# Cross attention whose shift rows carry the logarithm of the row sums, with the order of the work written out anew

## The chip, the core and the metric

The kernel runs on one core of a Trainium2 chip. The metric is the device time of one execution in microseconds (us), the median over runs. The core's engines work side by side, each through its own list of instructions, strictly in the order of that list: TensorE (PE in the rows; PEld is its loading of weights), VectorE (DVE), ScalarE (ACT), GpSimd (POOL) and SyncE (SP). They wait for one another through semaphores. A transfer is started ("issued") by an instruction in the list of SP or ACT and lands later.

## The reference

For 8 batches of 512 tokens with 512 features there are two blocks. The change is in the first, the cross attention over 77 context rows, with 16 heads of 32 features:

```python
q = (Q @ Wq).reshape(b, nq, H, dh).transpose(0, 2, 1, 3)      # Q = layernorm(x)
k = (K @ Wk)...; v = (V @ Wv)...                              # K = V = ctx_1024
S = einsum('bhqd,bhkd->bhqk', q, k) / sqrt(dh)
S = where(key_pos < valid_lens, S, -1e20)
A = softmax(S, axis=-1)
O = einsum('bhqk,bhkd->bhqd', A, v)
x = x + O.reshape(b, nq, d) @ Wo
```

The second block is a self attention over the 512 tokens, whose q, k, v and output weights get a low-rank part picked by a gate for each batch (two of eight experts); its result is added to x as well. Everything is float32.

## The kernel before

**The order.** Every piece of work is a step with a name and indices: `("csc", b, i, t)` is the cross scores of batch b, head group i, token tile t. A table, `CALENDAR` (L43 to L104), gives each kind of step a time for each of its indices; the step of batch b lies at `b * PERIOD + time`, with a period of 2034 units. A second table, `OWN` (L109 to L255), overrides single steps, mostly of the first and of the last batch. All steps are sorted by these times (`calendar`, L282), and each engine walks the sorted list and issues its part of each step (`Engine.walk`, L479). So the tables decide the order on each engine and nothing else; the units are not microseconds. Since three batches are under way at once, a step of batch b at time t lies among steps of batch b-1 at t + 2034 and of batch b-2 at t + 4068. The banks of PSUM and the slots of buffers are dealt out in the same order (`banks`, `ring`, L414 to L455).

**Cross attention of one batch** goes by four head groups i, of four heads each:

- `q1` (4 products) makes q; `q1_split` (ACT, DVE) splits it into a rounded part and a rest, so that the products that follow can run in the faster rounded format; `q1_rows` (ACT) and `q1_stack` (SP's transfers) put the parts under each other in a stack of rows (`cross_stack`, L584), one below the other: parts of q, a mask row, two shift rows.
- `csc` (L1255), four token tiles t: TensorE multiplies stack by keys, tokens on partitions, 4 heads x 78 columns; DVE takes the negated maximum of each row (L1040) into `negmax`.
- `cross_shift` (L1285): TensorE transposes `negmax`; DVE splits the 16 rows into a rounded part and a rest (L1051); `cross_shift_move` (L907): ACT issues two transfers that put them as shift rows under the stack.
- `csT` (L1292): TensorE multiplies again, now with keys on partitions, 99 rows deep, so that mask and maximum are already subtracted by the product itself; ACT takes the exponential into `probs1` (L914).
- `cpv` (L1305): probabilities by values, four products side by side on 32 columns each. `cden` (L1315): the same product with ones in place of the values, which gives the row sums on the partitions where the result stands.
- `cacc` (L928, ACT) copies the result out; `cinv` (L1078, DVE) takes the reciprocal of the row sums in four parts; `cdivide` (L757, POOL) multiplies the two, in one piece for i = 0 to 2 and in four for i = 3.
- `out1` (L1234): product with Wo, which waits for `cdivide`; `residual1` (L1084) adds it to x. Then come the second layer norm, the transposes `xpose`, the gate and the self attention: `weff`, `qk`, `v`, `sc`, `shift`, `shift_move`, `sT`, `pv`, `psum`, `den`, `inv`, `divide`, `out2`.

The self attention has shift rows of the same kind (`shift`, `shift_move`), and divides at the end (`den`, `inv`, `divide`). The two kinds of reciprocal share a ring of two buffers `inv_sum`. The score banks `sc` and `scT` have two buffers each, shared by cross and self attention, and the next score product in a bank waits until DVE or ACT has read the one before. `warm` steps multiply something that nobody reads, in the first batch alone.

Of the kernel before, what the change touches and what calls it, by code (L numbers as in the profile page):

```python
# [28 lines left out]
ROWS = SHIFT_ROW + 2  # L29
SIDE = 32  # L30
# [5 lines left out]
PJ_BANKS = 3  # L36
JUNK = 8
# [18 lines left out]
    "pick": (326,),
    "uv_load": (346, 397, 524, 2882),
    "csc": (-1491, -1471, -1462, -1458, -1042, -1041, -1018, -1014, -706, -696, -678, -673, -324, -308, -296, -277),
    "cross_shift": (-1369, -1007, -613, -257),
    "cross_shift_move": (-1320, -990, -595, -190),  # L60
    "csT": (-1253, -1237, -1208, -1190, -922, -921, -912, -880, -538, -500, -494, -473, -138, -137, -127, -84),
    "cpv": (-1128, -692, -415, -47),
    "cacc": (-1106, -626, -363, -44),
    "cden": (-963, -556, -444, -35),
# [1345 lines left out]
```

## Time and profile before

| | |
|---|---|
| median of 3 runs | 1420.75 us (1419.51 to 1426.21) |
| span of the profiled execution | 1426.7 us |
| TensorE busy | 1391.0 us, 97% |
| VectorE, ScalarE, GpSimd busy | 67%, 60%, 48% |
| mean granted TensorE clock | 0.98 of full |
| time from one batch to the next, batches 2 to 6 | 163.8 to 164.0 us |

The span of the profiled execution is 5.95 us longer than the median and 0.5 us longer than the longest of the three runs. How to read the rows further below: busy time is the time in which at least one instruction of a group runs, so the groups of TensorE, whose products overlap in the pipeline, sum to more than the engine's own busy time. A line of TensorE's products counts a float32 product as two records. The chain of waits goes back from the last instruction, at each step to what released it.

### The profile page before, as it was taken

The numbers are of one execution on the slowest core, as the hardware profiler recorded it, in microseconds if no ns is written. First come the engines' busy times: TensorE is split into PE (matmuls) and PEld (weight loads), VectorE is DVE, ScalarE is ACT, GpSimd is POOL, SyncE is SP. The second block draws the span as 40 slices with busy tenths as digits, with TensorE's granted clock in tenths as the row PEclk, the third lists the DMA queues.
The fourth block names the chain that finished last, engine by engine and source line by source line (L and its number), as shares of the span: only waits on it lengthen the run. The fifth ranks groups of instructions, "written<-read, shape, count | busy, mean of one in ns | idle before, by whom it ended". The sixth has DMA issues, their size and how long they took to land.

```text
span 1426.7 us, 17122 instructions
## 1 busy us (share of the span) xinstructions
PE 1391.0 (97%) x5704; PEld 702.4 (49%) x5704; DVE 951.9 (67%) x1687; ACT 861.3 (60%) x1499; POOL 679.8 (48%) x411
## 2 busy tenths in 40 slices
PE   8998999999999999999999999999999999999987
PEld 5545444545455444555555445455545454444432
DVE  4454577766767677767777677767777677666572
ACT  2425474866577663975658664876648665565652
POOL 2011143545555362556445463555625455465675
PEclk9889999999999999999999999999999999999999
DMA  7514233522434224522234224332235323233210
GB/s 252 143 53 133 46 68 96 153 76 46 98 110 108 75 54 125 137 61 76 68 111 123 75 59 135 110 85 67 58 104 152 76 46 97 64 101 79 81 39 30
DMA packets 78767, 130.81 MB, mean 92 GB/s; under 512 B 26374, under 2 KB 32134, under 8 KB 75607
## 3 DMA queue, kind: packets, MB, share of 16 engines
q1 hardware_dynamic: 74007, 128.55, 33.4%
q10 hardware_dynamic: 4672, 1.17, 0.4%
q8 instruction: 45, 0.74, 0.2%
q14 instruction: 43, 0.35, 0.1%
HBM read 66.08 MB, written 12.21 MB: 55 GB/s over the span
## 4 chain that ended last, share of the span: by engine, by line
PE 85%; ACT 7%; issue 2%; DMA 2%; POOL 2%; DVE 1%; ACTq 0%; SPq 0%; POOLq 0%
PE pj L1217 43%; PE scT L1302 9%; PE sc L1274 8%; PE acc L1331 7%; PE sc L1263 4%; PE pj L1247 2%; PE pj L1311 2%; PE scT L1295 2%; PE pj L1319 2%; PE pj L1340 2%; DMA qs<-shift 2%; PE pj L1190 1%; ACT xhat L810 1%; PE pj L1202 1%; PE pj L1211 1%
## 5 line engine op out<-in xcount | busy, mean ns | idle before, releaser
L925 ACT ACTIVATE probs<-scT 128x512 f32<-128x512 f32 x512 | 288.9, 594 | 303.9 <-PE scT L1302 300.8
L1048 DVE TENSOR_REDUCE negmax<-sc 128x1 f32<-128x512 f32 x512 | 338.0, 684 | 140.7 <-PE sc L1274 139.7
L784 POOL TENSOR_TENSOR probs_sum<-probs_sum,probs 128x1024 f32<-128x1024 f32 x128 | 300.2, 2365 | 57.4 <-ACT probs L925 57.3
L1075 DVE RECIPROCAL inv_sum<-pj 128x128 f32<-128x128 f32 x256 | 225.0, 921 | 59.9 <-PE pj L1340 39.2
L1274 PE MATMUL sc<-ks,qs 96*128 96x512 f32 x512 | 260.1, 541 | 2.4 <-DVE negmax L1048 1.6
L1217 PE MATMUL pj<-XT,Wqk 128*128 128x512 f32 x512 | 257.3, 598 | 0.6 <-DVE Wqk L1140 0.6
L1302 PE MATMUL scT<-qs,ks 99*128 99x512 f32 x512 | 250.9, 517 | 6.2 <-DMA qs<-shift 3.2
L780 POOL TENSOR_TENSOR probs_sum<-probs 128x1024 f32<-128x1024 f32 x64 | 151.4, 2372 | 173.8 <-ACT probs L925 173.8
L790 POOL TENSOR_TENSOR uv_stack<-UVS_sb,uv_stack 96x1024 fp32r<-96x1024 f32 x32 | 75.7, 2367 | 178.1 <-ACT UVS_sb L832 178.1
L1302 PEld LDWEIGHTS scT<-qs,ks 99*128 99x128 f32 x512 | 94.7, 191 | 124.5 <-ACT probs L925 60.4
L754 POOL TENSOR_TENSOR xhat<-xhat,inv_sum 128x128 f32<-128x128 f32 (+1 forms) x56 | 45.1, 806 | 207.7 <-DVE inv_sum L1075 207.7
L1274 PEld LDWEIGHTS sc<-ks,qs 96*128 96x128 f32 x512 | 97.9, 192 | 92.0 <-issue 47.1
L1331 PE MATMUL acc<-probs,V 128*32 128x512 f32 x1024 | 137.2, 613 | 0.0
L1217 PE MATMUL pj<-Wvo,ctx2T 128*128 128x512 f32 x256 | 131.0, 602 | 0.7 <-POOL ctx2T L754 0.7
L1217 PE MATMUL pj<-XT,Wq_sb 128*128 128x512 f32 x256 | 127.2, 601 | 1.1 <-ACT XT L844 1.1
L914 ACT ACTIVATE probs<-scT 77x512 f32<-77x512 f32 x128 | 72.4, 588 | 91.2 <-PE scT L1295 91.0
L1217 PE MATMUL pj<-Wvo,XT 128*128 128x512 f32 x256 | 122.4, 600 | 0.0
L1217 PEld LDWEIGHTS pj<-XT,Wqk 128*128 128x128 f32 x512 | 95.2, 191 | 54.7 <-issue 35.4
L1217 PE MATMUL pj<-Wo_sb,xhat 128*128 128x512 f32 x256 | 115.8, 599 | 0.0
L1263 PEld LDWEIGHTS sc<-keys,qsc 97*128 97x128 f32 x480 | 66.1, 196 | 34.5 <-issue 23.5
L893 ACT ACTIVATE ks<-stage_hi 32x512 fp32r<-32x512 f32 x128 | 80.1, 626 | 3.3 <-ACT stage_hi L868 0.6
L893 ACT ACTIVATE qs<-stage_hi 32x512 fp32r<-32x512 f32 x128 | 80.2, 626 | 2.7
(103 smaller groups left out, 1716.6 us busy)
## 6 DMA issues: line engine op xcount, KB each, us to landing
Wqk<-in_WmT SPq DMA_DIRECT2D x16, 1024.0 KB, 6.1
Wvo<-in_WmT SPq DMA_DIRECT2D x16, 1024.0 KB, 6.5
UVS_sb<-in_UVS SPq DMA_DIRECT2D x64, 192.8 KB, 3.4
qs<-stage_lo SPq DMA_DIRECT2D x136, 64.0 KB, 2.2
qs<-qs SPq DMA_DIRECT2D x34, 256.0 KB, 3.0
X<-in_x SPq DMA_DIRECT2D x8, 1024.0 KB, 6.0
ks<-stage_lo SPq DMA_DIRECT2D x128, 64.0 KB, 2.0
ks<-ks SPq DMA_DIRECT2D x32, 256.0 KB, 3.0
```

Source lines behind the costliest of these rows:

```text
L780: nc.gpsimd.tensor_tensor(probs_sum[:, pair], probs[:, 0, pair], probs[:, 1, pair], ALU.add)\
L784: nc.gpsimd.tensor_tensor(probs_sum[:, pair], probs_sum[:, pair], probs[:, kt % 2, pair], ALU.add)\
L790: nc.gpsimd.tensor_tensor(uv_stack[:].rearrange("p s n -> p (s n)"), UVS_sb[:, n, 0:2 * D], uv_stack[:].rearrange("p s n -> p (s n)").bitc ...
L893: nc.scalar.activation(stack[0:DH, slot, jj, :], stage_hi[jj * DH:(jj + 1) * DH, n, :].bitcast(F32), ACT.Copy).then_inc(sems["rows_copied" ...
L925: nc.scalar.activation(probs[:, kt % 2, jj, :], scT[:, ST[step], :], ACT.Exp, scale=SCALE)\
L1048: nc.vector.tensor_reduce(negmax[:, 0, n:n + 1], sc[:, SC[step], :], AX.X, ALU.max, negate=True)\
L1075: nc.vector.reciprocal(inv_sum[:, INV[use], at], pj[:, PJ[left_in(full)], at])\
L1217: mm = nc.tensor.matmul(pj[:, p, :], lhsT, rhs, start=(dc == 0), stop=(dc == DC - 1))
L1263: mm = nc.tensor.matmul(sc[:, SC[step], j * NKP:(j + 1) * NKP], cross_stack(b, i)[0:MASK_ROW + 1, j, t * P:(t + 1) * P], keys1[0:MASK_ROW ...
L1274: nc.tensor.matmul(sc[:, SC[step], :], qs[0:3 * DH, slot, jj, t * P:(t + 1) * P], ks[0:3 * DH, slot, jj, :], start=True, stop=True).then_i ...
L1302: nc.tensor.matmul(scT[:, ST[step], :], ks[0:ROWS, slot, jj, kt * P:(kt + 1) * P], qs[0:ROWS, slot, jj, :], start=True, stop=True).then_in ...
L1331: mm = nc.tensor.matmul(acc[jj * DH:(jj + 1) * DH, 0, :], V2[:, kt, v_slot(b, j), jj * DH:(jj + 1) * DH], probs[:, kt % 2, jj, :], start=( ...
```

## The change

Softmax is written as exp(s - max - ln(sum)), so the cross attention's second score product can give probabilities that are already divided. Per batch and head group i:

- added, for each token tile t: `cless` (DVE), scores minus row maximum, from PSUM into a buffer `lessened` of two slots (128 x 312); `cexp` (ACT), its exponential in place; `csum` (DVE), the sum over 77 keys. Once per group: `cln`, the logarithm of the 16 row sums per partition (ACT) and its scaling into the second half of `negmax`'s columns (DVE).
- `cross_shift` waits for `cln` instead of the last row maximum; the transpose is the same instruction and now gives 32 rows instead of 16. `cross_shift_move` issues four transfers instead of two. `csT` multiplies 101 rows instead of 99.
- the bank of a `csc` is free after `cless` instead of after the row maximum.
- removed: `cden` (4 products), `cinv` (4 reciprocals), `cdivide` (7 multiplications per batch on POOL). `out1` waits for `cacc` instead.
- the reciprocals of the self attention have one buffer (`INVERSES = 1`) where both kinds shared two. `hiddenB` lies in `xhat`, so the first `normalize` of the next batch waits for `gate_top`.
- ACT loads the table set `natural_log_exp_and_others` once at its start.
- both tables of times are new throughout; `PERIOD` is the same.

```diff
+CROSS_ROWS = SHIFT_ROW + 4
+INVERSES = 1
+LESS_SLOTS = 2
 CALENDAR = {
...
+    "q1": (-1643.9, -1643.8, -1643.7, -1643.6, -1620.7, -1620.6, -1595.8, -1593.3, -898.6, -898.5, -898.4, -844.5,
+        -785.4, -733.5, -700.9, -675.2),
+    "csc": (-1499, -1498.8, -1425.6, -1425.5, -1023.4, -1023.3, -999.2, -999, -704.4, -691.5, -664.1, -663.9,
+        -249.9, -249.8, -234.7, -234.5),
+    "cross_shift": (-1273.7, -924.6, -590.2, -161.6),
+    "cross_shift_move": (-1273.6, -924.5, -590.1, -161.5),
+    "csT": (-1191.9, -1191.8, -1160.3, -1160.2, -852.3, -852.2, -837.8, -837.7, -514.4, -508.9, -508.8, -432.8,
+        -128.9, -128.8, -72.5, -72.4),
+    "cpv": (-1004.3, -649.3, -424.6, -71.9),
+    "cless": (-1498.9, -1498.6, -1409.4, -1409.2, -1023.2, -1023.1, -999.1, -998.8, -704.3, -691.4, -664, -663.8,
+        -247.4, -247.2, -234.6, -234.4),
+    "cexp": (-1498.7, -1498.4, -1409.3, -1409.1, -1023, -1022.9, -998.9, -998.7, -681.1, -672.6, -632.8, -632.7,
+        -247.3, -247, -215.7, -215.5),
+    "csum": (-1498.5, -1457.9, -1292.9, -1292.8, -1022.8, -1022.7, -998.6, -998.5, -681, -672.5, -632.6, -632.5,
+        -247.1, -246.9, -215.6, -215.4),
+    "cln": (-1292.7, -998.4, -590.3, -215.3),
+    "cacc": (-1004.2, -649.2, -424.5, -71.7),
+    "out1": (-72.1, -72, -71.8, -71.5, -20.3, -20.2, -20.1, -20, -244.7, -244.6, -126.4, -53.1, -14.1, -14, -13.9,
+        -13.8),
+    "weff": (440.4, 440.6, 440.8, 483.2, 660.4, 660.5, 701.6, 701.7, 783.8, 784, 784.3, 835.4, 3211.8, 3289.7,
+        3378.9, 3379),
+    "qk": (504.9, 524.3, 551, 594.9, 732.1, 732.2, 732.3, 732.4, 1083, 1083.1, 1083.2, 1181.6, 1203, 1203.1, 1223,
+        1277, 1433.2, 1433.3, 1445.4, 1445.5, 1510.7, 1525, 1541.7, 1661.7, 2058.7, 2078, 2078.1, 2195.8, 2269.3,
+        2296.2, 2296.3, 2302.6),
+    "qk_rows": (892.3, 784.1, 1323, 1372.3, 1878.2, 1835.3, 2256.3, 2359.7),
+    "v": (786.9, 787, 857.2, 857.3, 799.1, 930.2, 930.3, 930.4, 979.9, 980, 980.1, 980.2, 997.1, 997.2, 1045.4,
+        1045.5),
+    "sc": (1116.5, 1116.6, 1165.3, 1165.4, 1183.3, 1183.4, 1200.7, 1200.9, 1221.8, 1221.9, 1231.5, 1248.8, 1248.9,
+        1295.3, 1295.4, 1328.9, 1502.5, 1502.6, 1511.6, 1577.8, 1577.9, 1650.4, 1650.5, 1673.4, 1673.5, 1742.2,
+        1839.3, 1839.4, 1897.4, 1897.5, 1954.6, 1954.7, 2011.8, 2011.9, 2051.3, 2051.4, 2134, 2134.1, 2223.1,
+        2259.3, 2259.4, 2295.7, 2295.8, 2299.6, 2299.7, 2310.7, 2310.8, 2331.3, 2459.3, 2459.4, 2493.6, 2493.7,
+        2550.6, 2550.7, 2565.6, 2603.6, 2748.1, 2748.2, 2783.4, 2783.5, 2819.5, 2819.6, 2873, 2873.1),
+    "shift": (1395.9, 2011.6, 2373.8, 2896.2),
+    "shift_move": (1426.6, 2011.7, 2373.9, 2896.3),
+    "sT": (1453.3, 1453.4, 1508, 1508.1, 1511.5, 1560.8, 1560.9, 1588.3, 1670, 1670.1, 1700.3, 1700.4, 1767.8,
+        1767.9, 1809.8, 1809.9, 2019.7, 2019.8, 2035.8, 2035.9, 2043.1, 2043.2, 2072.5, 2072.6, 2148.1, 2148.2,
+        2201.1, 2201.2, 2236.6, 2236.7, 2256.1, 2256.2, 2442.5, 2442.6, 2466.3, 2466.4, 2516.7, 2516.8, 2565.9,
+        2566, 2640.1, 2640.2, 2717.9, 2718, 2791.9, 2792, 2817.7, 2817.9, 2967.2, 3053.7, 3053.8, 3084, 3084.1,
+        3127.6, 3127.7, 3211.3, 3211.4, 3239.9, 3240, 3280.6, 3280.7, 3318.7, 3356.8, 3356.9),
+    "pv": (1603.5, 1603.6, 1881.7, 2042.9, 2089.7, 2236.5, 2341.2, 2341.3, 2640, 2698.3, 2800.8, 2935.1, 3157.1,
+        3277.4, 3440.2, 3440.3),
+    "den": (1890.5, 2381.3, 2937.2, 3444.2),
+    "out2": (3522.9, 3523, 3610.7, 3610.8, 3592.9, 3715.6, 3715.7, 3788.7, 3866.9, 3867, 3867.1, 3867.2, 3933.1,
+        3933.2, 3933.3, 3933.4),
...
 }
...
-        shift = sb("shift", [SIDE + HJ * TT, 2, P], F32R)
+        shift = sb("shift", [2 * SIDE, 2, P], F32R)
+        lessened = sb("lessened", [P, 2, HJ, NKP])
+        cross_sums = sb("cross_sums", [P, HJ * TT])
-        hiddenB = sb("hiddenB", [P, P])
+        hiddenB = xhat[:, 0, 0:P]
...
+        def scores_left(engine, step):
+
+            if step[0] == "csc":
+                return "cross_lessened", engine.after("cross_lessened", "cless", *step[1:])
+            return "rowmax_done", engine.after("rowmax_done", *step)
...
-            def cdivide(step, b, i, piece):
-                pool.wait_ge("pj_left_by_act", pool.after("pj_left_by_act", "cacc", b, i))
-                divided(step, ctx1T, "c", b, i, piece)
...
+            nc.scalar.preload_act_table_set("natural_log_exp_and_others")
...
             def cross_shift_move(step, b, i):
-                move_shift(1, cross_stack(b, i), "cross_shift_moved", b, ("cross_shift", b, i))
+                dst = cross_stack(b, i)
+                for part, split in enumerate(("shift_hi", "shift_lo")):
+                    act.wait_ge(split, act.after(split, "cross_shift", b, i))
+                    for side in range(2):
+                        row, at = SHIFT_ROW + 2 * side + part, SIDE + side * HJ * TT
+                        queue.dma_start(dst[row:row + 1].rearrange("p j (t n) -> p (j t) n", n=P).bitcast(F32),
+                                        shift[at:at + HJ * TT, part, :].bitcast(F32)).then_inc(sems["cross_shift_moved"], 16)
+
+            def cexp(step, b, i, t):
+                act.wait_ge("cross_lessened", act.after("cross_lessened", "cless", b, i, t))
+                at = lessened[:, LESS["cless", b, i, t]]
+                nc.scalar.activation(at, at, ACT.Exp, scale=SCALE).then_inc(sems["cross_exped"], 1)
+
+            def cln(step, b, i):
+                before = (b, i - 1) if i else (b - 1, DC - 1)
+                act.wait_ge("cross_scaled", act.after("cross_scaled", "cln", *before))
+                act.wait_ge("cross_summed", act.after("cross_summed", "csum", b, i, TT - 1))
+                nc.scalar.activation(cross_sums[:], cross_sums[:], ACT.Ln).then_inc(sems["cross_ln"], 1)
...
+            def cless(step, b, i, t):
+                if LESS_BEFORE[step]:
+                    dve.wait_ge("cross_summed", dve.after("cross_summed", *LESS_BEFORE[step]))
+                dve.wait_ge("rowmax_done", dve.after("rowmax_done", "csc", b, i, t))
+                scores = "csc", b, i, t
+                nc.vector.tensor_tensor(lessened[:, LESS[step]],
+                                        sc[:, SC[scores], 0:HJ * NKP].rearrange("p (j k) -> p j k", j=HJ),
+                                        negmax[:, 1, t:HJ * TT:TT].rearrange("p (j a) -> p j a", a=1).to_broadcast([P, HJ, NKP]),
+                                        ALU.add).then_inc(sems["cross_lessened"], 1)
+
+            def csum(step, b, i, t):
+                before = (b, i - 1) if i else (b - 1, DC - 1)
+                dve.wait_ge("cross_scaled", dve.after("cross_scaled", "cln", *before))
+                dve.wait_ge("cross_exped", dve.after("cross_exped", "cexp", b, i, t))
+                nc.vector.tensor_reduce(cross_sums[:, t:HJ * TT:TT], lessened[:, LESS["cless", b, i, t], :, 0:NK],
+                                        AX.X, ALU.add).then_inc(sems["cross_summed"], 1)
+
+            def cln(step, b, i):
...
+                nc.vector.tensor_scalar(negmax[:, 1, HJ * TT:2 * HJ * TT], cross_sums[:], -1.0 / SCALE, None, ALU.mult)\
+                    .then_inc(sems["cross_scaled"], 1)
...
-                pe.wait_ge("normed", pe.after("normed", "cdivide", b, dc, t * pieces(dc) // TT))
+                pe.wait_ge("pj_left_by_act", pe.after("pj_left_by_act", "cacc", b, dc))
...
-            def cden(step, b, i):
-                p = opened(left_in(step))
-                pe.wait_ge("exp_done", pe.after("exp_done", "csT", b, i, HJ - 1))
-                for j in range(HJ):
-                    mm = nc.tensor.matmul(pj[j * DH:(j + 1) * DH, p, :], ones[0:NK, :], probs1[0:NK, j, :],
```

## Rows read from the trace of the kernel before

**Rows 1.** The page, part 1: busy time of each engine, share of the span.

```profile
PE 1391.0 (97%) x5704; PEld 702.4 (49%) x5704; DVE 951.9 (67%) x1687; ACT 861.3 (60%) x1499; POOL 679.8 (48%) x411
```

**Rows 2.** Busy time by stretch: stretch, length, each engine's busy us, clock, DMA.

```profile
0.00:225.56 225.56, 212.06 (x814) 115.75 (x814) 123.45 (x226) 102.00 (x171) 46.40 (x40) 0.92 0.41 115
...
717.00:880.80 163.80, 162.88 (x691) 82.47 (x691) 116.19 (x205) 106.97 (x187) 84.06 (x50) 1.00 0.35 92
...
1208.60:1426.70 218.10, 201.99 (x760) 91.96 (x760) 130.83 (x216) 117.91 (x207) 129.01 (x71) 0.95 0.25 69
```

**Rows 3.** The chain that ended last: by line, then one piece: start, length, what.

```profile
by line: PE pj L1217 42.8%; PE scT L1302 8.7%; PE sc L1274 7.5%; PE acc L1331 7.2%; PE sc L1263 3.8%; issue 2.4%; PE pj L1247 2.3%; PE pj L1311 2.2%; PE scT L1295 2.2%; PE pj L1319 2.1%; PE pj L1340 1.6%; DMA qs<-shift 1.6%; PE pj L1190 1.3
...
557.45 8.59 PE pj L1217 x20
```

**Rows 4.** TensorE by line and shape: `cden` alone.

```profile
L1319 PE MATMUL pj<-probs,ones 77*32 77x512 f32 x256 | 35.5, 627 | 0.8 <-ACT probs L914 0.8
```

**Rows 5.** TensorE in order of time, batch of 553 to 717: start, length, instruction.

```profile
569.32 0.39 PE L1274 MATMUL sc<-ks,qs 96*128 96x512 f32 x1
569.55 0.40 PE L1302 MATMUL scT<-qs,ks 99*128 99x512 f32 x1
...
646.54 1.06 PE L1319 MATMUL pj<-probs,ones 77*32 77x512 f32 x8
647.42 1.04 PE L1331 MATMUL acc<-probs,V 128*32 128x512 f32 x8
...
679.70 1.06 PE L1319 MATMUL pj<-probs,ones 77*32 77x512 f32 x8
680.70 0.73 PE L1302 MATMUL scT<-qs,ks 99*128 99x512 f32 x2
```

**Rows 6.** VectorE by line and shape: busy us, mean ns, idle before.

```profile
L1075 DVE RECIPROCAL inv_sum<-pj 128x128 f32<-128x128 f32 x256 | 225.0, 921 | 59.9 <-PE pj L1340 39.2 <-PE pj L1319 18.3 <-POOL ctx2T L754 1.9
L1040 DVE TENSOR_REDUCE negmax<-sc 128x4 f32<-128x312 f32 x128 | 59.3, 477 | 30.3 <-PE sc L1263 29.8
...
L1151 DVE TENSOR_TENSOR V<-pj,vb_sb 128x384 f32<-128x384 f32 x12 | 6.6, 550 | 2.5 <-PE pj L1217 2.5
...
L1151 DVE TENSOR_TENSOR V<-pj,vb_sb 128x256 f32<-128x256 f32 x16 | 5.9, 417 | 5.0 <-PE pj L1217 2.5 <-PE acc L1331 2.4
...
L1018 DVE TENSOR_SCALAR vareps<-meanvar 128x4 f32<-128x4 f32 x16 | 2.7, 170 | 0.5
```

**Rows 7.** ScalarE by line and shape.

```profile
L893 ACT ACTIVATE qs<-stage_hi 32x512 fp32r<-32x512 f32 x128 | 80.2, 626 | 2.7
...
L914 ACT ACTIVATE probs<-scT 77x512 f32<-77x512 f32 x128 | 72.4, 588 | 91.2 <-PE scT L1295 91.0
...
L940 ACT ACTIVATE hidden<-pj,gb_sb 128x1 f32<-128x1 f32 x8 | 2.1, 261 | 3.4 <-PE pj L1349 2.6
L810 ACT ACT_TABLE_LOAD x1 | 1.3, 1283 | 2.8 <-issue 2.8
```

**Rows 8.** GpSimd by line and shape: the `cdivide` multiplications.

```profile
L754 POOL TENSOR_TENSOR xhat<-xhat,inv_sum 128x512 f32<-128x512 f32 x24 | 30.6, 1275 | 97.9 <-DVE inv_sum L1075 97.9
...
L754 POOL TENSOR_TENSOR xhat<-xhat,inv_sum 128x128 f32<-128x128 f32 x32 | 14.5, 454 | 109.9 <-DVE inv_sum L1075 109.9
```

**Rows 9.** Shift rows' transfers on ACT's queue: issue in ns (min/median/max), landing.

```profile
L900 ACTq DMA_DIRECT2D qsc<-shift x60: 510/601/1560, 49.9 to 1197.6; - x60
...
DMA to landing us min/median/max: 1.8/2.0/4.5
```

**Rows 10.** From the transpose (PE) to the issue (ACT's queue), in order of time.

```profile
643.44 0.27 PE L1280 MATMUL pj<-ident_sb,negmax 128*128 128x128 f32 x1
...
644.44 1.15 ACTq L900 DMA_DIRECT2D qsc<-shift  x2
```

**Rows 11.** Busy time by stretch, first batch, where the clock is lowest.

```profile
40.00:60.00 20.00, 19.13 (x89) 11.59 (x87) 8.84 (x19) 10.88 (x19) 0.00 (x0) 0.96 0.41 98
60.00:80.00 20.00, 19.23 (x82) 12.53 (x79) 11.05 (x18) 6.13 (x11) 1.27 (x1) 0.50 0.45 138
```

More of the change, by code:

```diff
@@ L56 @@
[L56 to L64, printed above, removed]
@@ L349, in increments @@
     if kind == "cross_shift_move":
-        return {"cross_shift_moved": 32}
+        return {"cross_shift_moved": 64}
     if kind in ("csT", "sT"):
         return {"scoresT_full": 1, "exp_done": 1}
-    if kind in ("cpv", "cden", "den"):
+    if kind in ("cpv", "den"):
         return {"pj_full": 1}
+    if kind == "cless":
+        return {"cross_lessened": 1}
+    if kind == "cexp":
+        return {"cross_exped": 1}
+    if kind == "csum":
+        return {"cross_summed": 1}
+    if kind == "cln":
+        return {"cross_ln": 1, "cross_scaled": 1}
     if kind == "cacc":
         return {"pj_left_by_act": 1}
-    if kind in ("cinv", "inv"):
+    if kind == "inv":
         return {"inverted": 1}
-    if kind in ("cdivide", "divide"):
+    if kind == "divide":
         return {"normed": 1}
@@ L434, in opens @@
 def opens(step):
-    return step[0] in ITSELF or step[0] in ("cpv", "cden", "den") or (step[0] in LEAVES and step[-1] == 0)
+    return step[0] in ITSELF or step[0] in ("cpv", "den") or (step[0] in LEAVES and step[-1] == 0)
 def banks(size):
@@ L454 @@
 STAGE, STAGE_BEFORE = ring([step for step in STEPS if step[0] in ("q1_split", "qk_split")], STAGES)
-INV, INV_BEFORE = ring([step for step in STEPS if step[0] in ("divide", "cdivide") and step[3] == pieces(step[2]) - 1], 2)
+INV, INV_BEFORE = ring([step for step in STEPS if step[0] == "divide" and step[3] == pieces(step[2]) - 1], INVERSES)
+LESS, LESS_BEFORE = ring([step for step in STEPS if step[0] == "cless"], LESS_SLOTS)
+LESS_BEFORE = {step: before and ("csum", *before[1:]) for step, before in LESS_BEFORE.items()}
 LEFT_BY = {"xpose": "pj_left_by_act", "gate_hidden": "pj_left_by_act", "cacc": "pj_left_by_act",
-           "cinv": "inverted", "inv": "inverted", "shift": "shift_lo", "cross_shift": "shift_lo"}
+           "inv": "inverted", "shift": "shift_lo", "cross_shift": "shift_lo"}
 class Engine:
@@ L805, in normalize @@
             def normalize(step, b, half):
-                before = ("out1", b, TT - 1, DC - 1) if half else ("xpose", b - 1, 1, TT - 1)
+                before = ("out1", b, TT - 1, DC - 1) if half else ("gate_top", b - 1)
                 act.wait_ge("pj_full", act.after("pj_full", *before))
```

272 lines of the change are left out of this document (131 added, 141 removed), and 211 rows, old and new, of tables (CALENDAR, OWN).

## The prediction

> **What bounds the kernel now.** First the page's busy times: TensorE runs 1391.0 of 1426.7 us, VectorE 952, ScalarE 861, GpSimd 680 [rows 1]. One engine leads by far, but an average can hide stages, so next the stretches. A middle batch takes 163.80 us with TensorE busy for 162.88 of them and every other engine under 117; five such batches lie between 163.65 and 164.00. Only the first stretch (225.56 us, TensorE 212) and the last (218.10, 201.99) have gaps [rows 2]. Busy need not mean full, since products overlap. So third the chain of waits: nearly all of it is TensorE, "issue" is 2.4% and a wait for shift rows 1.6%. Inside a piece of it 20 records of one line, ten products, take 8.59 us, 0.86 us each with nothing between [rows 3]. In order of time an `sc` and the `sT` behind it start 0.23 us apart [rows 5]. So in the middle the engine starts its next product as soon as it can, and time taken from its list comes off the period unless a new wait fills it. The Trainium skill (Trainium Kernel Development and Optimization, Performance Expectations) says that busy time of matmuls is a bad metric because they are pipelined, and that the busy share of weight loads is a good one; here that is 49%, and by this rule the engine would not be the bound. What follows if so is the third rival.
>
> **Removed from TensorE.** `cden`, 32 groups of 4 products. Its busy time is 35.5 us with 0.8 idle before it [rows 4], but part of that overlaps its neighbours. From its start to the start of what follows are 0.88 us in one place and 1.00 in another [rows 5], so 0.94 on the mean and 32 x 0.94 = 30.1; the chain gives the line 2.1% of 1426.7 = 30.0 us [rows 3]. Bounds: 32 x 0.86 = 27.5 (the time of one product step) and 35.5 + 0.8 = 36.3. I take 30.0, 3.75 per batch, because two readings meet there. Everything else that TensorE does has the same number of instructions; `csT` is two rows deeper and `cross_shift` is the same transpose, whose 32 rows cost nothing that a row shows.
>
> **VectorE.** Removed: 128 of 256 reciprocals, half of 225.0 us = 112.5. Added: 128 `cless`, between 417 ns for 256 columns and 550 for 384, so 475 for 312; 128 `csum`, as the maximum over the same 312, 477; 32 scalings at 170 [rows 6]. Together 127 us, so 14.8 more in all, 1.9 per batch: 118 of 164 us. **ScalarE.** Added: 128 `cexp`, between 261 ns for one element and 588 to 626 for 512, so about 0.48 for 312; 32 `cln` near 0.27 [rows 7]: 70 us, 8.8 per batch, on 107. Its queue issues 64 more transfers at 510 to 601 ns [rows 9], at most 38 us, 4.8 per batch. **GpSimd** loses 30.6 + 14.5 = 45.1 us [rows 8]. I cost these at nothing: TensorE's 162.88 us hide them, VectorE with 118 and ScalarE with 107 + 8.8 + 4.8 = 121 stay under a period of 160. Without that cover their order would count, which is the first rival.
>
> **The longer chain of a head group.** Before, `cross_shift` followed the last maximum. Now, for the last two tiles, VectorE does two maxima, two `cless` and two `csum` (2.86 us), one exponential (0.48), the logarithm (0.27) and the scaling (0.17) come in between, and six handovers. From the end of a transpose (643.71) to the first issue (644.44) are 0.73 us with one short VectorE copy of about 0.3 [rows 10], so 0.2 for a handover, 1.2 for six. The other exponential runs while VectorE sums. Chain: 5.0 us, less 0.5 because the first maximum runs while the second score product does: 4.5. What TensorE does meanwhile is read from the new calendar (a product step 0.86, `sc`, `sT` or `weff` 0.23, a side-by-side group 0.94). For i = 3, `csc` ends at -234.5 and `cross_shift` stands at -161.6; between them, one and two periods later in the table, lie two `sT` (1809.8, 1809.9), two `sc` (1839.3, 1839.4) and four `out2` (3866.9 to 3867.2): 4 x 0.23 + 4 x 0.86 = 4.4 us. For i = 1: two `v`, three `qk`, four `sT`: 5.2. For i = 0 and 2 in the same way 7.2 and 5.5. Against 4.5 the slack is 2.7, 0.7, 1.0 and -0.1.
>
> **Four transfers in place of two.** Transpose to first issue 1.0 us [rows 10], three more issues of 0.55, and 2.0 to land [rows 9]: 4.7, where it was 3.6. The covers from `cross_shift` to `csT` are 5.9, 6.0, 6.2 and 5.8 us (i = 1: four `sc`, four product steps, two `sT`, a `weff`, a `pv`): slack 1.1 to 1.5. The self attention's moves keep two transfers, 3.6 us; their covers become 6.4, 3.9, 4.4 and 5.0 (second: two `sc`, four `out1`): slack 2.8, 0.3, 0.8 and 1.4.
>
> **Waits with one answer.** A `csc` bank comes free one `cless` later (0.48), but pairs of `csc` lie 1.8 us of other work or more apart. One buffer of reciprocals: `inv` of a group waits for `divide` of the one before, which stands earlier in the table each time. `hiddenB` in `xhat`: `normalize` of the next batch stands at 238, `gate_top` at 237.9, and before the two followed each other as well. What is queued behind them on VectorE and ScalarE is no later for it. `cinv` and `cdivide` end no chain in the middle; without them `out1` waits for `cacc` (about 0.6) alone. Gate, picked weights and `weff` keep their place relative to `xpose`, and SP's loads follow the same steps: nothing. So in the middle I charge 0.5 us of new waits per batch (bounds 0 and 1.6, four places late by 0.4 each), 7 x 0.5 = 3.5, bounds 0 and 11.
>
> **First and last batch.** In the first the four groups have little beside them. Each gains the reciprocals and the division before `out1` (4 x 0.88 + 1.28 = 4.8 us [rows 6, 8]) and pays 4.0 + 1.1 for the longer chain. Net 0. Bounds: +10 if two such chains lie bare; -10 because 20 us of it run at a granted clock of 0.50, the lower of the two levels (1.2 of 2.4 GHz), behind 20 us at 0.96 in which TensorE was busy for 19.13 [rows 11], and a new order that keeps the clock up gets half of them back. The last batch's end hangs on `psum`, `den` and `out2`, which the change only reorders: 0, within 2 either way.
>
> **The sum.** -30.0 + 3.5 + 0 = -26.5. The profiled execution's 1426.7 is 5.95 longer than the median, so the difference is taken from the median: 1420.75 - 26.5 = 1394.
>
> **Rivals.** *First, slower:* ScalarE's order takes the place of the bound. Four row copies of 626 ns (`qk_rows`, `q1_rows`) in one block are 2.5 us [rows 7]. Where such a block stands ahead of a `cexp`, a `cln` or a move, that place is late by 2.5 less its slack: 5.9 us over the four chains, 4.9 over the cross moves, 4.9 over the self moves, 15.7 per batch. With a third of the places hit: 5.2 x 8 = 42, 1420.75 - 30 + 42 = 1433. It decides against the change from 3.75 us per batch on. For it: ScalarE waited for in order already gives the shift rows 1.6% of the chain [rows 3]. Against it: in the lists the blocks mostly stand where they begin well before.
>
> *Second:* logarithm and exponential do not stay loaded together, and each `cln` brings two loads of 1283 ns [rows 7]: 64 x 1.283 = 82 us on ScalarE. The chain is 5.8 instead of 4.5, which is short in three of four places, 2.3 us per batch, 18 in all; at most all 82 show. 1409 to 1473, middle 1441. The trace has a single load and says nothing of `Ln`. The Trainium skill (ScalarE: Activation LUTs, Table sets) says that one set holds both functions, so that no switch is needed; no run shows that yet.
>
> *Third, no change:* TensorE is not the bound, and 30 us leave it as idle time: 1421. The starts 0.86 and 0.23 us apart speak against it [rows 3, 5].
>
> *Fourth:* the clock in the first batch comes back: 1394 - 10 = 1384.
>
> **How the numbers follow.** Forecast, 1386 to 1405: 0.66. Fourth rival, below 1386: 0.07. New waits that eat 10 to 30 us, 1405 to 1428: 0.12, evenly. First rival 0.08, second 0.04, third 0.03. The range takes the low bound of first batch and end from the forecast (1394 - 12 = 1382), and upwards 27.5 removed, 11 of waits and 10 of first batch: 1414, 1416 with the end; it leaves out about 2 in 10. A measurement of this kernel can tell about 0.5%, 7 us. Faster: 0.66 + 0.07 + 0.06 = 0.79; same: 0.06 + 0.03 + 0.01 = 0.10; slower: 0.11.
>
> **What the changed profile would show.** Right: middle batches of 160 to 161 us, TensorE within 1.5 us of that, VectorE near 118, ScalarE near 116, no load of tables after the first. Wrong: waits of TensorE's weight loads for `csT` on transfers or for `cross_shift` on the scaled logarithm, over 3.75 us per batch (first rival); loads between `cln` and exponentials (second); batches of 164 with TensorE idle for 4 (third); a first stretch that differs from 225 by over 10.

## The result and the profile after

The changed kernel takes 1469.68 us (median of 4 runs, 1464.98 to 1471.64), the kernel before on the same chip 1423.48: a ratio of 1.032, interval 1.0285 to 1.0355. Forecast were 1394 and a range from 1382 to 1416. The profiled execution of the changed kernel took 1470.47 us, its span is 1468.7. First the page's busy times, which answer [rows 1]:

```profile
PE 1386.2 (94%) x5448; PEld 696.4 (47%) x5448; DVE 969.3 (66%) x1847; ACT 904.7 (62%) x1659; POOL 637.3 (43%) x355
```

TensorE lost 256 records, yet its busy time fell by 4.8 us only while the span grew by 42. Next the stretches, as in [rows 2], cut where the first `residual1` of a batch starts (stretch, length, busy us by engine, clock, DMA):

```profile
97.12:243.16 146.04, 130.25 (x446) 64.23 (x445) 86.51 (x168) 76.84 (x140) 28.40 (x17) 0.92 0.28 70
...
243.16:406.60 163.44, 160.74 (x659) 81.15 (x658) 118.26 (x230) 111.83 (x207) 78.86 (x43) 1.00 0.33 86
406.60:575.95 169.35, 162.94 (x659) 81.71 (x658) 118.52 (x229) 111.96 (x207) 78.83 (x43) 0.99 0.35 89
...
747.40:912.77 165.37, 160.76 (x659) 81.13 (x658) 118.05 (x225) 111.85 (x207) 78.86 (x43) 1.00 0.34 87
...
1251.76:1468.70 216.94, 194.20 (x743) 88.44 (x741) 126.06 (x214) 117.01 (x206) 127.36 (x67) 0.96 0.24 64
```

Of the six middle batches the first is as long as before (163.4 us), the other five take 165 to 171, with TensorE idle for 4.6 to 7.2 of them where it had been idle for 1. In the longer ones it is also busy longer at a lower clock (162.94 at 0.99, 160.76 at 1.00): the same products run slower. What TensorE waits for (us in all, times, longest; `qs<-shift` are the shift rows of the self attention, `qsc<-shift` those of the cross attention, `negmax` of L1168 is the scaled logarithm):

```profile
PE scT L1398 <- DMA qs<-shift: 30.8, 11, 9.6
PE pj L1376 <- DVE negmax L1168: 14.2, 9, 7.0
PE scT L1391 <- DMA qsc<-shift: 5.4, 6, 1.9
```

The largest is the **self** attention's shift rows, which the change does not touch. One of these waits in order of time (start, length, instruction):

```profile
909.83 0.40 SPq L726 DMA_DIRECT2D X<-in_x  x1
910.27 2.11 SPq L705 DMA_DIRECT2D keys<-k_hbm  x3
...
913.28 0.51 SPq L717 DMA_DIRECT2D V<-v_hbm  x1
913.43 0.27 PE L1376 MATMUL pj<-ident_sb,negmax 128*128 128x128 f32 x1
...
913.83 0.41 SPq L772 DMA_DIRECT2D Wvo<-in_WmT  x1
914.01 3.60 PE L1313 MATMUL pj<-Wo_sb,xhat 128*128 128x512 f32 x8
914.40 1.15 ACTq L962 DMA_DIRECT2D qs<-shift  x2
...
921.38 1.22 PE L1398 MATMUL scT<-qs,ks 99*128 99x512 f32 x2 [3.77 <-DMA qs<-shift]
...
922.39 3.62 PE L1313 MATMUL pj<-Wo_sb,xhat 128*128 128x512 f32 x4
```

The transpose, the split and the two issues come as quickly as in [rows 10] (1.0 us to the first issue). But SP has just issued the next X, keys, V1 and the value weights, and the rows are usable 7 us after their first issue; TensorE stands for 3.77 us. Ahead of the gap eight records of products take 3.60 us, behind it four take 3.62, so the clock has halved too. The transfers of 909 to 922 (KB each, us to landing):

```profile
Wvo<-in_WmT SPq DMA_DIRECT2D x1, 1024.0 KB, 8.0
...
qs<-shift ACTq DMA_DIRECT2D x2, 8.0 KB, 6.4
```

8 KB land in 6.4 us where [rows 9] had a median of 2.0 for the same kind of transfer. The gap comes back in five of the six middle batches, at 2.67 to 3.98 us; in the first of them, the one that is as long as before, it is 0.77. The last batch has it once more, behind the key weights, and there it is the longest:

```profile
1283.38 0.42 SPq L772 DMA_DIRECT2D Wqk<-in_WmT  x1
...
1284.19 1.17 ACTq L962 DMA_DIRECT2D qs<-shift  x2
...
1294.36 1.22 PE L1398 MATMUL scT<-qs,ks 99*128 99x512 f32 x2 [9.59 <-DMA qs<-shift]
```

The second wait belongs to the change. The scaling of 16 columns, all 32 of its instructions (ns min/median/max, first and last start):

```profile
L1168 DVE TENSOR_SCALAR negmax<-cross_sums x32: 165/176/6025, 49.7 to 1236.6; 128x16 f32<-128x16 f32 x32
```

Two of them in order of time, beside GpSimd:

```profile
222.52 6.03 DVE L1168 TENSOR_SCALAR negmax<-cross_sums 128x16 f32<-128x16 f32 x1 [0.34 <-ACT cross_sums L983]
223.58 4.93 POOL L830 TENSOR_TENSOR X<-X,ob_sb 128x512 f32<-128x512 f32 x4
...
978.88 2.37 POOL L851 TENSOR_TENSOR uv_stack<-UVS_sb,uv_stack 96x1024 fp32r<-96x1024 f32 x1 [0.54 <-ACT UVS_sb L893]
978.94 2.34 DVE L1168 TENSOR_SCALAR negmax<-cross_sums 128x16 f32<-128x16 f32 x1 [0.48 <-ACT cross_sums L983]
...
981.33 0.33 PE L1376 MATMUL pj<-ident_sb,negmax 128*128 128x128 f32 x1 [1.09 <-DVE negmax L1168]
```

GpSimd's operation ends at 981.25, the scaling at 981.28: 2.34 us for what takes 0.18 alone. This stands in six batches at the same place. (Seven more scalings take 0.75 to 0.89 us.) At 222.52 GpSimd runs operation behind operation until 228.51, and the scaling ends at 228.55. The third wait follows the four issues:

```profile
898.73 0.27 PE L1376 MATMUL pj<-ident_sb,negmax 128*128 128x128 f32 x1
...
900.66 2.46 ACTq L971 DMA_DIRECT2D qsc<-shift  x4
...
903.16 2.58 ACT L954 ACTIVATE qs<-stage_hi 32x512 fp32r<-32x512 f32 x4 [3.24 <-issue]
...
905.64 0.68 PE L1391 MATMUL scT<-qsc,keys 101*77 101x512 f32 x2 [0.69 <-DMA qsc<-shift]
```

### The profile page after: what moved, and what is told of

Same layout as the page of the kernel before. It is cut to its first block, busy times and chain, and to the rows that moved or that the text cites. A ratio compares the mean times of both kernels' runs of the same rounds, so it can differ in the third digit from the quotient of the medians.

```text
span 1468.7 us, 17077 instructions
## 1 busy us (share of the span) xinstructions
PE 1386.2 (94%) x5448; PEld 696.4 (47%) x5448; DVE 969.3 (66%) x1847; ACT 904.7 (62%) x1659; POOL 637.3 (43%) x355
## 4 chain that ended last, share of the span: by engine, by line
PE 74%; DVE 8%; DMA 7%; ACT 6%; issue 2%; ACTq 2%; POOL 1%; SPq 0%; DVEq 0%; POOLq 0%
PE pj L1313 38%; PE scT L1398 8%; PE acc L1419 7%; PE sc L1370 7%; DMA qs<-shift 4%; PE sc L1359 3%; DVE negmax L1124 2%; PE scT L1391 2%; PE pj L1407 2%; PE pj L1343 2%; DMA qsc<-shift 1%; DVE negmax L1168 1%; ACT xhat L871 1%; PE pj L1286 1%; ACTq L971 1%
## 5 line engine op out<-in xcount | busy, mean ns | idle before, releaser
L1001 ACT ACTIVATE probs<-scT 128x512 f32<-128x512 f32 x512 | 279.0, 593 | 281.0 <-PE scT L1398 245.7
L1124 DVE TENSOR_REDUCE negmax<-sc 128x1 f32<-128x512 f32 x512 | 330.6, 682 | 104.1 <-PE sc L1370 102.8
L1398 PE MATMUL scT<-qs,ks 99*128 99x512 f32 x512 | 223.9, 507 | 34.2 <-DMA qs<-shift 30.8
L1370 PE MATMUL sc<-ks,qs 96*128 96x512 f32 x512 | 215.5, 486 | 2.3 <-DVE lessened L1152 0.7
L813 POOL TENSOR_TENSOR rstd<-vareps,minus_half 128x4 f32<-128x4 f32 x16 | 16.3, 1018 | 290.3 <-DVE minus_mean L1095 290.3
L1313 PE MATMUL pj<-Wo_sb,xhat 128*128 128x512 f32 x256 | 128.7, 638 | 0.2
L1177 DVE RECIPROCAL inv_sum<-pj 128x128 f32<-128x128 f32 x128 | 108.7, 910 | 29.5 <-PE pj L1428 29.1
L823 POOL TENSOR_TENSOR ctx2T<-ctx2T,inv_sum 128x128 f32<-128x128 f32 (+1 forms) x56 | 44.4, 809 | 186.6 <-ACT ctx2T L1011 157.2
L1313 PE MATMUL pj<-Wvo,ctx2T 128*128 128x512 f32 x256 | 119.6, 594 | 0.7 <-POOL ctx2T L823 0.7
L977 ACT ACTIVATE lessened<-lessened 128x312 f32<-128x312 f32 x128 | 56.4, 461 | 48.8 <-DVE lessened L1152 42.2
```

The source lines that it names most:

```text
L1001: nc.scalar.activation(probs[:, kt % 2, jj, :], scT[:, ST[step], :], ACT.Exp, scale=SCALE)\
L1124: nc.vector.tensor_reduce(negmax[:, 0, n:n + 1], sc[:, SC[step], :], AX.X, ALU.max, negate=True)\
L1177: nc.vector.reciprocal(inv_sum[:, INV[use], at], pj[:, PJ[left_in(("den", b, j))], at])\
L1313: mm = nc.tensor.matmul(pj[:, p, :], lhsT, rhs, start=(dc == 0), stop=(dc == DC - 1))
L1370: nc.tensor.matmul(sc[:, SC[step], :], qs[0:3 * DH, slot, jj, t * P:(t + 1) * P], ks[0:3 * DH, slot, jj, :], start=True, stop=True).then_i ...
L1398: nc.tensor.matmul(scT[:, ST[step], :], ks[0:ROWS, slot, jj, kt * P:(kt + 1) * P], qs[0:ROWS, slot, jj, :], start=True, stop=True).then_in ...
```

## The experiments

**Theory A**: the change is sound, and three things around it cost the time: loads ahead of the shift rows, the scaling stuck behind GpSimd, four issues. **Theory B**: the added chain and operations themselves are too late, and the waits are only where that shows. All runs, with the start of batch 1's `residual1`, the mean period from there to batch 7 and the rest (us of the profiled execution). The texts below call a run by the first part of its name (e3, e4 and so on). The runs lay on three chips, on which the kernel before took 1421.3 (e1 to e4), 1424.4 (e5 to e8) and 1422.5 (e9, e10); each ratio is to the kernel before on the same chip, and differences between runs of different chips carry these 3 us.

| kernel | median | ratio to before | to batch 1 | period | rest |
|---|---|---|---|---|---|
| before | 1423.5 | | 230.9 | 164.1 | 211.4 |
| after | 1469.7 | 1.032 | 243.2 | 168.1 | 216.9 |
| e3_no_division | 1396.3 | 0.982 (0.978 to 0.986) | 221.7 | 160.2 | 209.9 |
| e4_old_calendar | 1555.5 | 1.094 (1.090 to 1.099) | 273.7 | 178.4 | 209.6 |
| e1_loads_behind | 1454.7 | 1.023 (1.019 to 1.027) | 240.6 | 166.0 | 216.2 |
| e5_loads_behind_2 | 1444.0 | 1.012 (1.007 to 1.018) | 236.7 | 164.4 | 222.2 |
| e8_weights_behind | 1447.8 | 1.017 (1.013 to 1.022) | 238.3 | 165.1 | 217.4 |
| e7_loads_ahead | 1478.2 | 1.037 (1.034 to 1.041) | 227.6 | 172.5 | 215.7 |
| e2_scale_on_act | 1453.4 | 1.021 (1.016 to 1.026) | 234.8 | 166.7 | 215.9 |
| e9_two_issues | 1453.1 | 1.020 (1.016 to 1.025) | 230.3 | 166.8 | 217.2 |
| e10_loads_only_defect | 1435.8 | 1.009 (1.006 to 1.011) | 229.5 | 165.9 | 209.8 |
| e6_three_mended | 1413.0 | 0.993 (0.990 to 0.996) | 232.4 | 161.3 | 210.5 |

### What the removal is worth

Run e3:

```diff
+    times = {step: time for step, time in times.items() if step[0] not in ("cden", "cinv", "cdivide")}
...
-                pe.wait_ge("normed", pe.after("normed", "cdivide", b, dc, t * pieces(dc) // TT))
+                pe.wait_ge("pj_left_by_act", pe.after("pj_left_by_act", "cacc", b, dc))
```

> The kernel before, with its own calendar, without the denominator products of cross attention, their reciprocals and divisions, and with nothing put in their place: out1 takes the undivided context, so the output is not the reference's. It prices the removal alone. Theory A, with the step of the prediction that took 3.75 us per batch off TensorE: 1423 - 30 = 1393 us (1388 to 1400). Theory C (TensorE does not set the pace there, what is removed turns into waits): 1415 to 1423.

25 us off (1421.3 to 1396.3). The period falls by 3.9 us and a middle batch has TensorE busy for all but one:

```profile
702.37:862.52 160.15, 159.21 (x659) 81.68 (x658) 103.07 (x189) 106.89 (x188) 78.56 (x43) 1.00 0.35 94
```

So TensorE is the bound in the middle, and this is what the removal alone reaches in the old calendar. (The row is a stretch, as above.)

### The operations in the calendar of before

Run e4:

```diff
+        at = [times["csc", b, i, t] for t in FOUR]
+        for t in FOUR:
+            times["cless", b, i, t], times["cexp", b, i, t] = at[t] + 0.01, at[t] + 0.02
+            times["csum", b, i, t] = min(at[t] + 20, at[t + 2] + 0.005) if t < 2 else at[t] + 20
+        times["cln", b, i] = at[3] + 30
+        turn = times["cross_shift", b, i] = max(times["cross_shift", b, i], at[3] + 60)
```

> All operations of the changed kernel in the calendar of the kernel before: the new steps stand behind each score product (differences and exponentials at once, sums 1.6 us later, the logarithm 2.4 us behind the last score product), the cross transpose no less than 4.8 us behind the last score product and the scores' transposed products no less than 4.7 us behind that; all else, the loads too, where it was. Theory A (the calendar, not the operations, lost the time): the -30 of the removal less 0.5 to 1.5 us per batch for the chain, about 1400 us (1392 to 1412). Theory B (the added operations lose it wherever the calendar puts them): 1445 to 1475.

A miss: slower than anything expected of it. One head group, in order of time:

```profile
961.75 2.57 ACT L903 ACTIVATE ks<-stage_hi 32x512 fp32r<-32x512 f32 x4
...
964.35 0.46 ACT L926 ACTIVATE lessened<-lessened 128x312 f32<-128x312 f32 x1
...
964.72 2.57 ACT L903 ACTIVATE qs<-stage_hi 32x512 fp32r<-32x512 f32 x4
...
967.31 0.21 ACT L932 ACTIVATE cross_sums<-cross_sums 128x16 f32<-128x16 f32 x1
...
967.88 0.45 PE L1325 MATMUL pj<-ident_sb,negmax 128*128 128x128 f32 x1 [3.51 <-DVE negmax L1117]
```

A block of row copies stands ahead of the exponential and another ahead of the logarithm, 2.57 us each: the prediction's first rival, its 2.5 us per block. In all TensorE waits 34.2 us for the scaled logarithms and 27 for score banks that `cless` frees late. So the chain does not fit into the old calendar with these fixed distances; no other placement in it was tried. In the changed kernel's own calendar this does not happen, as e6 shows.

### Loads behind the shift rows

Run e1:

```diff
-    "context": (-2106.3,),
-    "context_v": (-2105.6,),
-    "load": (-2141.2,),
-    "stats": (-2047.5, -2047.4, -2047.3, -1843.8),
+    "context": (-2056.1,),
+    "context_v": (-2056,),
+    "load": (-2056.2,),
+    "stats": (-1844.1, -1844, -1843.9, -1843.8),
-    "wm_load": (162, 660.3, -59.6, 3079.7),
+    "wm_load": (162, 660.3, -22.2, 3079.7),
...
+                sp.wait_ge("shift_moved", sp.after("shift_moved", "shift_move", b - 2, 1))
```

> The changed kernel, with four steps of SyncE's list (the next X, keys, V1 and the value weights) put right behind the self-attention shift move of group 1 and made to wait until its two transfers have landed; the norm statistics of three tiles are put later so that VectorE does not stand before the X load. Theory A (these loads, issued 0.5 to 4.5 us ahead of the 8 KB shift rows, keep them from landing for some 6 us, and the product that waits 2.7 to 4.0 us for them drops TensorE's granted clock): the wait on the shift rows falls under 1 us in the middle batches and 9.6 us in the last to under 3, the period of the middle batches falls from 168.1 to about 163.5 us, the clock of each to 1.00, and the time to 1470 - 6 x 4.5 - 7 = about 1436 us (1425 to 1446). Theory B (the new chain and its operations take the time, the loads only stand near it): the same 1470 within 5, the wait being taken over by another.

The middle batches' waits on the rows go from 2.67 to 3.98 down to 0.25 at most, but only 15 us come back: the moved `stats` stand ahead of the gate's hidden vector on VectorE and make a product wait 1.4 us in each middle batch. With `stats` at (-1960, -1955, -1950, -1843.8), run e5:

> e1_loads_behind with the three norm statistics put 9 us earlier than there, out of the stretch ahead of the gate's hidden vector, where they had made a product wait 1.34 us on VectorE in each batch. Theory A (loads ahead of the shift rows cost what the waits and the lower clock show, and 1.3 us of each batch of e1 was this side effect): the period of the middle batches falls from 166.0 in e1 to about 164.6 us and the time to 1454.7 - 7 x 1.34 = about 1445 us (1440 to 1449). Theory B (something else takes its place): 1452 to 1456.

As theory A says, 26 us below the changed kernel. Not all of it is the loads' doing: by the table the six periods give back 22, ahead of batch 1 another 6.4 come back, most of them because the long scaling of 222.52 is missed (longest scaling 2341 ns, not 6025), and the last stretch is 5.3 longer. The wait behind the key weights stands in that stretch as it did (9.60 us, 9.59 in the changed kernel); TensorE is busy longer there at a lower clock (199.12 at 0.93, 194.20 at 0.96). With the value weights alone behind the rows, run e8:

> The changed kernel, with only the value weights (1 MB, the last of the four loads and the nearest to the rows, 0.57 us ahead of the first issue) made to wait for the shift rows; the X load, the keys and V1 stay ahead of them. Theory A with the nearest load as the cause: the wait on the rows falls to under 1.5 us and the time is that of e5, about 1445 us. Theory A with the whole group as the cause: the rows still wait for what is left of the X load and the keys, 1.5 to 3 us, and the time is 1455 to 1463. Theory B: 1467 to 1472.

One middle batch of e8 in order of time:

```profile
735.36 1.15 ACTq L963 DMA_DIRECT2D qs<-shift  x2
...
740.29 0.41 SPq L773 DMA_DIRECT2D Wvo<-in_WmT  x1
...
740.31 0.74 PE L1399 MATMUL scT<-qs,ks 99*128 99x512 f32 x2 [1.75 <-DMA qs<-shift]
```

The rows are in 4.9 us after their issue; the waits are 1.73 to 1.98, the size expected if the whole group is the cause. Most of the time came back all the same (1447.8, where 1455 to 1463 had been expected): behind these shorter waits five of the six middle batches keep a granted clock of 1.00, where the changed kernel has it in two. From e6, this run and the changed kernel: with none, about 1.6 and about 2.6 MB of these loads issued just ahead, the rows take 2.5, 4.9 and 7.0 us from their first issue until they can be used.

The other way round, in the kernel before (run e7): the value weights and the context loads put just ahead of the move of group 2.

```diff
-    "context": (-2070,),
-    "context_v": (-1185,),
+    "context": (-1715.9,),
+    "context_v": (-1715.8,),
-    "wm_load": (235, 409, 224, 3285),
+    "wm_load": (235, 409, 318, 3285),
...
+                    sp.wait_ge("rowmax_done", sp.after("rowmax_done", "sc", b - 1, 2, TT * HJ - 2))
```

> The kernel before, with the value weights, the keys and V1 (1.0 MB and two smaller loads) issued just ahead of the self-attention shift move of group 2, when the next-to-last score tile of the group is reduced; nothing else is changed. Theory A: the cause planted in the other kernel costs the same there, a wait of 2.5 to 4 us on the shift rows in each batch, the granted clock at 0.98 to 0.99 and the period at 166.5 to 169.5 instead of 163.85: 1421 + 7 x 3 to 5.5 = 1442 to 1460 us. Theory B (loads do not delay the rows; the chain of the change does): 1419 to 1425.

54 us slower, more than expected. The wait that was to appear did (1.65 to 3.44 us in the middle), in order of time:

```profile
771.83 0.37 SPq L705 DMA_DIRECT2D Wvo<-in_WmT  x1
...
776.76 1.15 ACTq L901 DMA_DIRECT2D qs<-shift  x2
...
782.85 0.73 PE L1303 MATMUL scT<-qs,ks 99*128 99x512 f32 x2 [2.09 <-DMA qs<-shift]
...
783.72 0.29 ACT L823 ACTIVATE s_signed<-stack_rows_sb,UVS_sb 96x2 f32<-96x2 f32 x1 [6.58 <-DMA UVS_sb<-in_UVS]
```

The last line is a second effect that I had not priced: in SP's list the picked experts' rows stand behind the waiting load, ScalarE stands 6.58 us for them, and the exponentials behind make TensorE wait another 2.8 us. So e7 shows that loads ahead of the rows make them late in the other kernel too, not what that costs; the price is e5's and e10's to give.

### The scaling on ScalarE

Run e2:

```diff
+                nc.scalar.activation(negmax[:, 1, HJ * TT:2 * HJ * TT], cross_sums[:], ACT.Copy, scale=-1.0 / SCALE)\
+                    .then_inc(sems["cross_scaled"], 1)
...
-                nc.vector.tensor_scalar(negmax[:, 1, HJ * TT:2 * HJ * TT], cross_sums[:], -1.0 / SCALE, None, ALU.mult)\
-                    .then_inc(sems["cross_scaled"], 1)
```

> The changed kernel, with the 128x16 multiplication of the logarithms made by ScalarE right behind the logarithm, not by VectorE. Theory A' (VectorE's small multiplication ends only when a running GpSimd operation ends: 2.34 us in each batch and 6.03 us once where its median is 0.17): the waits of the cross transpose on the multiplication, 1.1 us in each of six batches and 7.0 us once, go to 0.3 or less each, and the time to 1470 - 6 x 0.9 - 6 = about 1459 us (1454 to 1463). Theory B (the chain is late as a whole and its last link only shows it): 1470 within 3, with the same wait put down to ScalarE.

16 us less, where about 11 had been expected (ns min/median/max of the operation there):

```profile
L986 ACT ACTIVATE negmax<-cross_sums x32: 215/215/217, 48.2 to 1220.3; 128x16 f32<-128x16 f32 x32
```

None of 32 is stretched, and TensorE waits 1.6 us for it in place of 14.2. So the chain was not late as a whole.

### Two issues in place of four

Run e9:

```diff
-                    for side in range(2):
-                        row, at = SHIFT_ROW + 2 * side + part, SIDE + side * HJ * TT
-                        queue.dma_start(dst[row:row + 1].rearrange("p j (t n) -> p (j t) n", n=P).bitcast(F32),
-                                        shift[at:at + HJ * TT, part, :].bitcast(F32)).then_inc(sems["cross_shift_moved"], 16)
+                    row = SHIFT_ROW + 2 * part
+                    queue.dma_start(dst[row:row + 2].rearrange("p j (t n) -> p (j t) n", n=P).bitcast(F32),
+                                    shift[SIDE:2 * SIDE, part, :].bitcast(F32)).then_inc(sems["cross_shift_moved"], 16)
```

> The changed kernel, with only the cross rows moved in two issues of two rows each in place of four of one row. Theory C (ScalarE's queue stands some 3 us in four issues, and the last of them lands after the product wants it): the wait of the transposed cross products on the rows, 0.7 to 1.9 us in each batch, goes to 0.2 or less, and ScalarE's exponentials behind it come 1.2 us sooner; 1470 - 7 x 0.8 = about 1463 us (1459 to 1466). Theory B (slack, ScalarE waits for TensorE anyway): 1468 to 1472.

The wait goes (0.4 us once), the period falls by 1.3 (0.8 had been expected). The 13 us more come ahead of batch 1. Of these, 8.3 lie behind the first `residual1` of batch 0: there the scaling met GpSimd's row of operations, and a slightly earlier order misses it (longest scaling 2341 ns, not 6025; e5 likewise). That part is luck of timing, and e2 takes it too. The other 4.6 lie ahead of it, where the changed kernel has a wait of 2.35 us on rows that go in four issues and a granted clock of 0.84, e9 no such wait and 0.89; no run parts the two.

### All of it, and all but the loads

Run e6:

> All of it together, on the changed kernel: the loads behind the shift rows with the statistics of e5; the key weights of the last batch, too, behind the shift move of group 2 (they stand 0.8 us ahead of the rows that land 7.9 us later in the changed kernel); the multiplication on ScalarE as in e2; and the four issues of the cross rows made two, each with the rows of both sides (rows in the order maximum high, logarithm high, maximum low, logarithm low). Theory A (three separate causes, the waits add): middle periods of 164.6 - 1.1 - 0.7 - clock = 161.5 to 162.8 us, the first 235 us as in e2, the end 209 to 212: 1445 - 16 - 7 - 5 = about 1417 us (1408 to 1426). Theory B (new waits follow): 1430 to 1440.

Run e10:

> e6_three_mended with the four loads (X, keys, V1, value weights) put back ahead of the shift rows of group 1, and the statistics with them; the multiplication on ScalarE, the two issues and the key weights of the last batch stay mended. If the causes add, it gives back what the loads cost alone, 26 us between the changed kernel and e5: 1413 + 26 = about 1439 us (1433 to 1445), periods of 165 to 169 us with 2.5 to 4 us of wait on the rows. If the loads only hurt a chain that is late already: 1415 to 1430.

e6, which moves the key weights of the last batch behind the rows of group 2 as well, is at 1413.0, 57 us below the changed kernel and by a small margin below the kernel before (0.993, interval 0.990 to 0.996), with middle batches like this one:

```profile
716.18:877.17 160.99, 160.10 (x659) 81.13 (x658) 114.81 (x221) 112.94 (x211) 78.79 (x43) 1.00 0.36 94
```

The loads and the rows in the same kernel, in order of time:

```profile
878.80 1.21 ACTq L967 DMA_DIRECT2D qs<-shift  x2
...
881.27 0.40 SPq L777 DMA_DIRECT2D Wvo<-in_WmT  x1
...
881.44 1.03 PE L1399 MATMUL scT<-qs,ks 99*128 99x512 f32 x2
```

With the loads alone put back (e10; the three statistics go back with them) 22.8 us are lost again, 26 had been expected. A middle batch of e10 as a stretch, and its wait on the rows (us in all, times, longest):

```profile
725.10:890.05 164.95, 161.47 (x659) 81.98 (x658) 114.75 (x221) 112.82 (x211) 78.80 (x43) 0.99 0.36 92
...
PE scT L1396 <- DMA qs<-shift: 24.9, 10, 4.3
```

For the middle batches theory A stands and theory B falls: the same operations in nearly the same calendar, with four loads and the statistics, one small operation and the issues placed otherwise, run at TensorE's pace. Ahead of batch 1 theory B is not ruled out: there e6 takes 10.7 us more than e3, and no run takes that apart.

## Why the prediction was wrong, step by step

- **What bounds the kernel: right.** e3 takes the products out and the period follows, 3.9 us for a forecast of 3.75. In all it is 25.0, not 30.0. The third rival fell: the weight loads are busy for 50% of e3's span, and TensorE idles for under 1 us in a middle batch all the same. The sentence of the Trainium skill (Trainium Kernel Development and Optimization, Performance Expectations) from which I drew it is about closeness to roofline, not about which engine bounds a kernel.
- **"SP's loads follow the same steps: nothing": the step that failed.** The loads do follow the same steps, but in the new calendar they stand right ahead of a shift move. I did not read SP's list at the places that I had given 0.3 us of slack, and none of the signs of being wrong that I had listed names these rows. In place of nothing, the rows come 7.0 us after their first issue, TensorE waits 2.67 to 3.98 us for them in five middle batches, and its clock falls behind most of these waits. The term is 23 us (e10 against e6) to 26 (e5); by the six periods alone 27 and 22.
- **"2.0 to land": failed as a constant.** [Rows 9] had a longest landing of 4.5 us, and I took the median. At 7.0 us from issue to product, no cover of the self moves (3.9 to 6.4 us) would have held.
- **The scaling at 0.17 us: right as a median, wrong where it matters**, 2.34 us in six batches and 6.03 once. The price came from another small operation, whose mean of 170 ns shows no such case [rows 6]. The Trainium skill (SBUF — State Buffer, Who interferes with whom) says that this kind of operation can take a read and write port pair which VectorE shares with GpSimd, and that the later one then fully blocks. This trace agrees: 2.34 us against 0.18, GpSimd's operation 0.06 us ahead, both ending together. I had not weighed it.
- **Four transfers, slack 1.1 to 1.5: failed for i = 3.** The wait there is 0.68 to 1.93 us. From transpose to first issue are 1.93 us instead of 1.0, because VectorE is at other work (a residual and two maxima); the four issues take 2.46, and the product starts at 905.64, 6.9 us behind the transpose where 4.7 was forecast. The gain of e9 in the period, 1.3 us, is the term.
- **The longer chain at 4.5 us, new waits 0.5 per batch: right for the middle once the rest is mended.** In e6 the period is 161.3, 1.1 above e3. Nearly all of that is not waiting: over the six batches TensorE is busy for 961.6 us in e6 and 955.7 in e3, and idle 6.2 and 5.4. So the new waits are 0.1 us per batch, and 1.0 is a term that I had put at nothing: TensorE is busy longer with as many products. Whether the deeper `csT` or the new order does it no run shows. Hence the first rival did not come true in this calendar; e4 shows what it looks like when it does.
- **First batch 0, within 10: missed.** +12.2 us to batch 1, of which 7.0 are the stuck scaling. A quarter of the records of `cden` lies in that stretch (64 of 256), 7.5 of the 30 us, so with the removal the forecast for it was -7.5. e3, without the chain, has -9.2 and e6 +1.5: what is added costs 10.7 there, where I had 5.1. **End 0, within 2: missed**, +5.5, with the 9.59 us behind the key weights in it; in e6 -0.9. No run moves the key weights alone; e10, which does so beside the scaling and the issues, ends in 209.8 where e2 and e9 take 215.9 and 217.2.
- **Operations and table loads: right.** VectorE is busy 118 us per middle batch (118), ScalarE 112 (116; issues do not count as busy), and the table is loaded once, so the second rival fell.

From the median: 25.0 removed, 16.7 that e6 keeps over e3, 56.7 for loads, scaling and issues (after against e6): 1421.3 - 25.0 + 16.7 + 56.7 = 1469.7. The sum closes because its terms are differences of runs; it proves nothing by itself. In the profiles e6 keeps 17.9 over e3: 10.7 ahead of batch 1, 6.7 in the middle and 0.5 at the end. Alone the three mends give back 26, 16 and 17, but the stuck scaling of the first batch is in all three, so these do not simply add. What the loads cost in the six middle batches of e10 against e6, 27.4 us, is for 16.5 idle time of TensorE and for 10.9 longer busy time at a lower clock.

## What to carry to other kernels

When an order of work is written anew, check each short transfer on the critical path for what the other queue issues in the microseconds ahead of it; a large load without a near deadline can wait on the small one's semaphore. Price a small operation by its longest case beside the engine that it may meet, not by its median. Pack rows that go the same way into one transfer, since the issuing engine stands for each.

## What the runs showed that I had not expected

- Two transfers of 8 KB on ScalarE's queue take 2.5, 4.9 and 7.0 us to be usable with none, about 1.6 and about 2.6 MB of the four loads just ahead, and up to 9.6 us to land in the last batch, though the queues differ. The Trainium skill (DMA: Bandwidth & Descriptors, Issuing engines are not separate DMA queues) says that they run on the same 16 engines and interleave; here the rows come near the end of the loads rather than between them (6.4 us, value weights 8.0).
- A waiting VectorE operation can be passed over by several GpSimd operations that follow each other: 6.03 us at 222.52, through one that ran already and the four of 223.58.
- Behind two gaps of different length the clock differs. The stretches after the waits of 3.77 and 2.67 us in the changed kernel (as the stretches above):

```profile
921.40:926.00 4.60, 4.60 (x7) 2.35 (x8) 0.00 (x0) 1.08 (x2) 0.00 (x0) 0.50 0.00 0
...
754.90:760.00 5.10, 5.10 (x20) 2.35 (x20) 0.96 (x3) 1.68 (x4) 0.00 (x0) 1.00 0.00 0
```

TensorE is busy throughout both. Behind the longer wait it runs at the lower level (1.2 GHz) and gets 7 records done, behind the shorter at 2.4 GHz and 20. Behind the other three waits of 3.61 to 3.98 us the next 4.6 us have a granted clock of 0.63 or 0.64, behind the one of 0.77 us 1.00.
